# Differential attention, one head group at a time or overlapped across head groups, and its causal mask on TensorE or on GpSimd

## What is computed

```
def causal_attn_pair(q, k, v1, v2, mask, scale):
    s = jnp.einsum('bthd,bshd->bhts', q, k) * scale
    s = jnp.where(mask, s, NEG)
    a = jax.nn.softmax(s, axis=-1)
    o1 = jnp.einsum('bhts,bshd->bthd', a, v1)
    o2 = jnp.einsum('bhts,bshd->bthd', a, v2)
    return jnp.concatenate([o1, o2], axis=-1)
```

## Time and profile before

| | us |
|---|---|
| median of three runs | 4769.63 (4766.91 to 4773.21) |
| profiled execution: time | 4766.31 |
| profiled execution: span | 4764.7 |
| of it, differential attention | about 2130 to 3024 |
| one iteration of it | 54.45 |

### The profile page before, as it was taken

The page is one execution under the profiler, slowest core; times in us unless marked ns, Lnnn a source line. Parts: engine busy times, 40 slices in busy tenths (PEclk is TensorE's granted clock), DMA queues, the critical chain, the costliest instruction groups (busy, mean ns, idle before and its releaser), DMA issues. The chain is left out here.

```text
span 4764.7 us, 168106 instructions
## 1 busy us (share of the span) xinstructions
PE 3911.8 (82%) x69376; PEld 2562.6 (54%) x69376; DVE 2238.0 (47%) x6160; ACT 1304.5 (27%) x4110; POOL 382.9 (8%) x829
## 2 busy tenths in 40 slices
PE   8788888888888888879999999576999979488830
PEld 4377777777777777764444444333333334244410
DVE  2155555555555555545555555233666633221224
ACT  1033333333333333322223333122444411011100
POOL 0000000000000000000000000000000004300034
PEclk9999999999999999999999999788999979799975
DMA  2230000000000000000100000201111111287866
GB/s 67 48 147 0 0 0 0 0 0 0 0 0 0 0 0 0 0 22 31 46 31 31 31 31 31 74 18 42 60 62 46 46 49 67 90 258 240 256 175 157
DMA packets 144600, 256.56 MB, mean 54 GB/s; under 512 B 25943, under 2 KB 76375, under 8 KB 142516
## 3 DMA queue, kind: packets, MB, share of 16 engines
q1 hardware_dynamic: 118516, 201.96, 13.1%
q0 software_dynamic: 21248, 53.30, 4.0%
q10 hardware_dynamic: 4800, 0.81, 0.1%
HBM read 147.95 MB, written 62.92 MB: 44 GB/s over the span
## 5 line engine op out<-in xcount | busy, mean ns | idle before, releaser
L305 PE MATMUL gru_pr<-gru_whh,h 128*4 128x128 f32 x16384 | 544.4, 274 | 229.8 <-DVE h L396 229.8
L305 PEld LDWEIGHTS gru_pr<-gru_whh,h 128*4 128x4 f32 x16384 | 388.9, 87 | 373.3 <-DVE h L396 367.1
L305 PE MATMUL gru_pz<-gru_whh,h 128*4 128x128 f32 x16384 | 541.7, 273 | 2.3 <-issue 2.3
L305 PE MATMUL gru_pn<-gru_whh,h 128*32 128x128 f32 x16384 | 541.6, 273 | 0.0
L305 PEld LDWEIGHTS gru_pn<-gru_whh,h 128*32 128x32 f32 x16384 | 458.4, 110 | 1.3
L305 PEld LDWEIGHTS gru_pz<-gru_whh,h 128*4 128x4 f32 x16384 | 438.9, 87 | 9.9 <-issue 2.4
L376 DVE STREAM_TRANSPOSE gru_tr<-gru_pr 128x128 f32<-128x128 f32 x512 | 162.2, 317 | 379.7 <-PE gru_pr L305 379.7
L340 ACT ACTIVATE gru_rn<-gru_pre 128x16 f32<-128x16 f32 x512 | 118.5, 231 | 706.9 <-DVE gru_pre L378 706.9
L389 DVE STREAM_TRANSPOSE gru_tz<-gru_pz 128x64 f32<-128x64 f32 x1024 | 194.8, 228 | 121.3 <-PE gru_pz L305 121.3
L530 ACT ACTIVATE da_probT<-da_ps 128x1024 f32<-128x1024 f32 (+3 forms) x256 | 180.1, 703 | 195.4 <-PE da_ps L501 194.1
L280 POOL COPY gru_pick<-ident 128x4 f32 x512 | 95.9, 187 | 1687.5 <-PE gru_pz L296 1682.2
(11 more groups left out here) (270 smaller groups left out, 5521.7 us busy)
## 6 DMA issues: line engine op xcount, KB each, us to landing
ex_wg<-in_L_ffn_gate_up_proj SPq DMA_DIRECT2D x64, 768.0 KB, 5.3
ex_wd<-in_L_ffn_down_proj SPq DMA_DIRECT2D x64, 384.0 KB, 6.1
xg<-gru_zeros SPq DMA_DIRECT2D x4, 4096.0 KB
da_hb<-wide SPq DMA_DIRECT2D x16, 1024.0 KB, 4.7
fa_hb<-xnT SPq DMA_DIRECT2D x16, 1024.0 KB
ex_xg<-xg SPq DMA_DIRECT2D x64, 256.0 KB, 2.7
eo<-ex_eo POOLq DMA_DIRECT2D x64, 256.0 KB, 6.3
da_wg<-ahead SPq DMA_DIRECT2D x48, 256.0 KB, 4.8
```

Source lines behind the costliest of these rows:

```text
L305: last = nc.tensor.matmul(rows(j), of(c), whh[:, c, g, j, :], start=(c == 0 and start), stop=(c == KD - 1))
```

## The change

The class `AttentionCore` goes, and `diff_attention_stage` holds its own loops. The first iteration and the last are written out, and a loop runs the fourteen between.

- The first pass goes in 16 half steps of two heads. Two sets of two banks (0, 1 and 2, 3) alternate.
- Between the half steps of iteration `it` PE now does the key sums and output transposes of `it - 1` and the projections of queries and keys, and their swaps, for `it + 1`. The values of `it + 1` are projected in four slices within the second pass. ACT and DVE get the pieces that go with them at the same places: normalisation of `it - 1` on DVE stands behind the fourth half step's maximum, the rotations behind the third running sum, the halves of the keys ahead of the last.
- The maxima are added to `q`, in a row that the masked half leaves free, with -1 in the matching row of `kp`. The matmul with -1 (L497), `top` and its rounding go.
- The mask matmul of the second pass (L501) goes. After each exponential of two heads POOL sets the masked part of the 128x128 diagonal block of each to zero, in place (`affine_select` on 128x2x128 of `probT`). The weighing of values and the running sum wait for that (`kept`) where they waited for `exp_done`.
- Values pass through a second buffer (`vn` to `v`), and the products through `pv`. The idle matmuls of `keep_warm` go in this stage.

```diff
...
+            sp.sem_inc(v_done, 1)
             with sp.Fori(0, B) as b:
                 with sp.Fori(0, KD) as g:
 
-                    sp.wait_ge(w_free, b * KD + g + 1)
+                    sp.wait_ge(v_done, b * KD + g + 1)
...
+            def times_cosine(j):
                 for n in (1, 0):
-                    pool.wait_ge(raw, it * 2 + (2 - n))
+                    pool.wait_ge(rotated, j * 2 + 1)
+                    pool.wait_ge(raw, j * 2 + (2 - n))
                     nc.gpsimd.tensor_tensor(cc[:, n, :], qk[:, n, :], cs[:, 0, :], ALU.mult).then_inc(cosed, 1)
+
+            def keep_causal(it, n):
+                for half_of in range(2):
+                    block_of = probT[:, n % 2, 2 * half_of:2 * half_of + 2, groups[n][0] * P:(groups[n][0] + 1) * P]
+                    pool.wait_ge(exp_done, it * HV + (2 * n + half_of + 1))
+                    pool.sem_inc(seen, 1)
+                    nc.gpsimd.affine_select(block_of, block_of, [[0, 2], [1, P]], ALU.is_ge, 0.0, base=0,
+                                            channel_multiplier=-1).then_inc(kept, 1)
+
+            def iteration(it, first=False, last=False):
+                if not last:
+                    times_cosine(it + 1)
+                for n in range(NG):
+                    keep_causal(it, n)
+
+            times_cosine(0)
+            over_iterations(pool, iteration)
...
+            def project(j, n, ks, first=False):
+                if ks[0] == 0:
+                    if n == 1:
+                        pe.wait_ge(hb_in, j * 64 + 64)
+                    if not first:
+                        pe.wait_ge(pv_kept, j * 1 + (-1))
...
+            def score_for_max(it, m):
+                i, a = queries[m // 2]
+                L = (i + 1) * P
+                heads = (2 * (m % 2), 2 * (m % 2) + 1)
+                if m in (0, 2):
+                    pe.wait_ge(q_ready, it * 2 + (a + 1))
+                    pe.wait_ge(keys_ready, it * 2 + (a + 1))
+                if m >= 2:
+                    pe.wait_ge(max_done, it * HV + (m - 1))
+                for h in heads:
+                    nc.tensor.matmul(ps[:, h, 0:L], q[slots[h], a, i * P:(i + 1) * P], kp[slots[h], a, 0:L], start=True, stop=False)
+                for h in heads:
+                    last = nc.tensor.matmul(ps[:, h, i * P:L], identb[:], maskb[:], start=False, stop=True)
+                last.then_inc(scored, 1)
+
+            def sum_exponentials(it):
+                for a in range(2):
+                    pe.wait_ge(added, it * NG + (NG - 1 + a))
+                    for h, sl in enumerate(slots):
+                        last = nc.tensor.matmul(ps[sl, BSUM + a, :], ones[:], total[:, a, h, :], start=True, stop=True)
...
+            def score_keys(it, n):
+                kt, a = groups[n]
+                q0 = kt * P
+                if n < 2:
+                    pe.wait_ge(q_topped, it * 2 + (a + 1))
+                for half_of in range(2):
+                    if n:
+                        pe.wait_ge(exp_done, it * HV + (2 * n - 1 + half_of))
+                    heads = (2 * half_of, 2 * half_of + 1)
+                    for h in heads:
+                        last = nc.tensor.matmul(ps[:, h, q0:T], kp[slots[h], a, kt * P:(kt + 1) * P], q[slots[h], a, q0:T],
+                                                start=True, stop=True)
+                    last.then_inc(keys_scored, 1)
...
+            def weigh_values(it, n):
+                kt, a = groups[n]
+                q0 = kt * P
+                pe.wait_ge(kept, it * HV + (2 * n + 2))
+                for h, sl in enumerate(slots):
+                    last = nc.tensor.matmul(ps[sl, BPV + a, q0:T], v[:, kt, sl], probT[:, n % 2, h, q0:T],
...
+            def iteration(it, first=False, last=False):
+                j = it + 1
+
+                def maxima(m):
+                    score_for_max(it, m)
+                    score_for_max(it, m + 1)
+
+                maxima(0)
+                if not first:
+                    sum_exponentials(it - 1)
+                maxima(2)
+                if not last:
+                    project(j, 1, (0, 1), first)
+                maxima(4)
+                if not last:
+                    project(j, 1, (2, 3))
+                maxima(6)
+                if not last:
+                    project(j, 0, (0, 1), first)
+                maxima(8)
+                if not last:
+                    project(j, 0, (2, 3))
+                    swap_pairs(j, 1)
+                maxima(10)
+                if not first:
+                    output(it - 1)
+                maxima(12)
+                maxima(14)
+                if not last:
+                    swap_pairs(j, 0)
+                maxima_to_rows(it, first)
+                for n in range(NG):
+                    score_keys(it, n)
+                    if n < TT and not last:
+                        if n == 0:
+                            pe.wait_ge(q_topped, it * 2 + 1)
+                        project_v(j, n)
+                    if n == 1:
+                        pe.wait_ge(v_set, it * 1 + 1)
+                        if not last:
+                            pe.wait_ge(sined, j * 2 + 2)
+                        else:
+                            pe.wait_ge(pv_kept, it * 1)
+                    if n:
+                        weigh_values(it, n - 1)
+                weigh_values(it, NG - 1)
+
...
+            def halves_of_q(j):
+                act.wait_ge(rotated, j * 2 + 3)
+                for a in range(2):
+                    nc.scalar.activation(q[:, a, :], rot[:, 0, :], ACT.Copy, scale=half[:, a:a + 1]).then_inc(q_ready, 1)
+
+            def keep_v(j):
+                act.wait_ge(v_done, j * 1 + 2)
+                act.wait_ge(v_set, j * 1)
+                nc.scalar.activation(vn[:].rearrange("p t d -> p (t d)"), ps[:, BV, :], ACT.Copy).then_inc(vn_ready, 1)
+
+            def move_v(j):
+                act.wait_ge(vn_ready, j * 1 + 1)
+                nc.scalar.activation(v[:].rearrange("p t d -> p (t d)"), vn[:].rearrange("p t d -> p (t d)"), ACT.Copy).then_inc(v_set, 1)
...
+            def exponentials(it, n):
+                kt, a = groups[n]
+                q0 = kt * P
+                if n >= 2:
+                    act.wait_ge(product, it * NG + (n - 1))
+                    act.wait_ge(added, it * NG + (n - 1))
+                for half_of in range(2):
+                    heads = slice(2 * half_of, 2 * half_of + 2)
+                    act.wait_ge(keys_scored, it * HV + (2 * n + half_of + 1))
+                    nc.scalar.activation(probT[:, n % 2, heads, q0:T], ps[:, heads, q0:T], ACT.Exp, scale=scale).then_inc(exp_done, 1)
+
+            def keep_products(it, first=False):
+                act.wait_ge(product, it * NG + NG)
+                if not first:
+                    act.wait_ge(scaled, it * 2)
+                nc.scalar.activation(pv[:], ps[:, BPV:BPV + 2, :], ACT.Copy).then_inc(pv_kept, 1)
+
+            def iteration(it, first=False, last=False):
+                j = it + 1
+                if not first:
+                    move_v(it)
+                    reciprocal(it - 1)
+                if not last:
+                    keep_raw(j, 1)
+                    keep_raw(j, 0)
+                if not first:
+                    keep_output(it - 1)
+                for n in range(NG):
+                    if n == 0 and not first:
+                        act.wait_ge(added, it * NG)
+                    exponentials(it, n)
+                    if n == TT and not last:
+                        keep_v(j)
+                if not last:
+                    act.wait_ge(keys_scored, it * HV + HV)
+                    halves_of_q(j)
+                keep_products(it, first)
+
+            keep_raw(0, 1)
...
+            def rotate(j, n):
+                dve.wait_ge(sined, j * 2 + (2 - n))
+                dve.wait_ge(cosed, j * 2 + (2 - n))
+                dve.wait_ge(q_ready, j * 2)
+                dve.wait_ge(keys_ready, j * 2)
+                nc.vector.tensor_tensor(rot[:, n, :], sw[:, n, :], cc[:, n, :], ALU.add).then_inc(rotated, 1)
+
+            def halves_of_keys(j):
+                dve.wait_ge(rotated, j * 2 + 2)
+                for a in range(2):
+                    nc.vector.tensor_scalar(kp[:, a, :], rot[:, 1, :], half[:, a:a + 1], half[:, 2 + a:3 + a],
+                                            ALU.mult, ALU.add).then_inc(keys_ready, 1)
...
+            def output(it):
+                dve.wait_ge(rec_done, it * 1 + 1)
+                nc.vector.tensor_tensor(err[:], ps[:, BSUM:BSUM + 2, :], rec[:], ALU.mult).then_inc(refined, 1)
+                dve.wait_ge(refined, it * 2 + 1)
+                nc.vector.scalar_tensor_tensor(rec[:], err[:], -2.0, rec[:], op0=ALU.add, op1=ALU.mult).then_inc(refined, 1)
+                dve.wait_ge(refined, it * 2 + 2)
+                dve.wait_ge(pv_kept, it * 1 + 1)
+                for a, o in enumerate((o1, o2)):
```

(94 more changed lines are left out.)

290 lines of the change are left out of this document (64 added, 226 removed).

## The result

The changed kernel took 4783.07 us (median of 20 runs, 4770.83 to 4822.28) against 4769.18 for the kernel before beside it. The ratio is 1.0034, 95% interval 1.0019 to 1.0049: slightly slower, and outside the predicted range of 4675 to 4775 us. The profiled execution has a span of 4786.9 us against 4764.7.

The account below looks back on a forecast made before the run. PE bounds each iteration: 45.6 us of work plus waits gives a 51.6 us period against 54.45. Fifteen periods gain 42.8, the last iteration 3.9, the first 0.6, in all 47: 4721 us, range 4675 to 4775.

Parts of the forecast that it names:

- PE's work: Differential attention, one iteration: PE's parts sum to 45.6 us against 54.45, the period if PE never waited.
- The sixteen half steps: First pass: two heads each, scores of mean 0.65 us plus mask matmuls of 0.22, sixteen times 0.87, 13.9 us.
- the moved pieces: Unchanged PE work: key sums 1.8 us, projections and swaps 8.8, values 3.6, output transposes 0.6, transposes of maxima 1.1.
- The waits: PE waits: 1.5 us behind DVE's output, 0.9 for last maxima and their use, 3.7 in the second half on POOL.
- The select: POOL's masking in the second pass, 16 an iteration: 0.55 us alone, bounds 0.40 and 0.73, up to 1.5 beside running sums.
- Its reading of two collisions: Earlier trace: a POOL multiplication and a DVE addition each stretched by 0.21 us, so the two engines were taken as exclusive.
- The rival of the clock: Without idle matmuls PE's clock falls; a tenth of the stage at half clock adds 42 us, 4763; 8% with a tie.
- a tie: Iterations do not overlap because one wait ties an iteration's head to its predecessor's tail; 8% together with the clock.
- the prediction's own signs of being wrong: Select alone over 0.9 us, half steps at 512 columns over 1.2, or DVE or ACT the engine that never waits.
- The last iteration: No projections, but a tail that no longer hides: walked at 45.5 us against 49.4, gain 3.9.
- The walk: Stepping through the new order with estimated durations to place waits: period 51.6 us, last iteration 45.5.
- The other side's rival: Slow select on POOL: decides from 0.9 us on; 4786 us at 1.0, 4890 at 1.4; chance 20%.

Follow-up runs that it names:

- the kernel without a mask: Changed kernel without the causal mask of the second pass (no select, part of the computation left out): 4685.9 us, ratio 0.9831.
- the output in pieces: Changed kernel with select in four groups, mask matmuls in the last four, DVE's output in three pieces, 6 idle matmuls per place in the last iteration: ratio 0.9840.

## Why the prediction was wrong

**PE's work: the sum right, its terms not.** 45.6 us forecast, 45.2 in the kernel without a mask, by errors that cancel. The second pass was put at 15.75 us and is 13.2 (2623.01 to 2641.19, less 4.4 of value projections and 0.6 of waits): the prediction took away the slots of L497 and L501 but left the halves of a group in sequence, as in the earlier trace rows. The sixteen half steps were put at 13.9 and take 14.7 (the sum of their slots in the iteration from 2594.02, at a clock of 1.00), and the moved pieces, forecast at 15.9 together, take 17.2 there.

**The waits: right.** For the select 4.0 against 3.7, behind DVE's output 1.0 against 1.5. The 3.7 came from a select of 0.55 us alone, which takes 0.41, so that it is so near is in part luck. Without the 4.1 us of clock the period is 54.6 - 4.1 = 50.5, between the forecast 51.6 and its bound with a select of 0.40 (4697, 24 us less in fifteen periods: 50.0).

**The select: the lower bound, with the port shared.** 0.41 us alone, and up to 1.77 beside DVE, where the prediction said 0.55 and up to 1.5. Its reading of two collisions (0.21 us each) was enough to find this. The Trainium skill ("SBUF — State Buffer", section "Who interferes with whom") says that of VectorE and GpSimd one is blocked while the other holds the port pair that they share; the row of four selects in 3.50 us agrees.

**The failed step** is "The idle matmuls go: they fill waits, and I cost their loss at nothing, since the granted clock is 1.00 in the iteration with waits of up to 1.2 us in it". That reading of the earlier trace rows was circular: the clock was 1.00 with the idle matmuls in the iteration, and the kernel before without them is 300 us slower. In the changed kernel waits of the same length, at most 1.2 us, and a total of 4.0 in the last groups, where what lies between them is short, were enough to halve the clock for the next 6 us and more. Two edits each gave it back: twelve idle matmuls among these waits, and mask matmuls in the last four groups, which take the waits away. It costs 4.1 us in each of thirteen periods, 53 us; the periods would else have come out 1.1 shorter than forecast, which gives 14 back. The rival of the clock was named with a chance of 8%, shared with a tie, and "4763 if a tenth of the stage ran at half clock": too rare and too small. Of the prediction's own signs of being wrong one came true, a half step at 512 columns of over 1.2 us (2.33). The stage had a granted clock of 0.91 in its middle iterations, with 25 us at 0.50 in the last.

**The last iteration** is the second term: 45.5 us forecast, 69.0 measured. The walk used the 1.5 us wait of a middle iteration, whose projections cover DVE's output; without them it is 4.2. That is 2.7 of the 23.5 us. Its opening at half clock, as in the other iterations, is 4.1. Then 25 us at 0.50, in which PE is busy for 21.7, lose some 11 more. Of the other 6 the last sums, at half clock once more, are 1.6 (3.48 us where 1.90 is the full-clock length); the rest I can't split. With the output in pieces and the clock held for the most part the iteration was still 56.7, with 36 idle matmuls in it whose slots sum to 8.2 us. Less these it is 48.5, so the walk itself was probably a few us short.

**The other side's rival** (a slow select) did not happen; slower came from the clock.

## To carry to other kernels

Idle matmuls are part of the schedule: before an edit removes them, ask what the granted clock is without them, since a row that shows it at full clock with them in place says nothing. A wait can cost more than its length, and did here where the work around it was narrow; put the cheap substitute (here the select) where wide matmuls cover it, and leave matmul work in the tail that would otherwise wait. An iteration peeled off a loop has to be walked on its own, with the work that is missing from it.

## What the hardware showed that I had not expected

- The clock's loss outlasts its cause: PE busy 2.62 of 6 us at the end of an iteration, then 6 us at 0.50 and 6 at 0.76 though PE was busy throughout. In the kernel before without idle matmuls it stayed at 0.50 for over 40 us of uninterrupted score, mask, weighing and sum matmuls (2600.30 to 2643), and came back in the projections (0.98 from 2643 to 2646).
- Two 128-column bf16 mask matmuls behind each half of the scores cost 1.38 us in the first group, at 512 columns, where their own slots are 0.34: they end the overlap of row strips.
- One and the same loop body ran at 51.3 us and then at 54.6 us in one execution (select in the order before); PE's waits were shorter in the slow iterations, the granted clock was lower.
